# The first norm of a Mamba and gated-MLP layer on Trainium2, formed with channels instead of tokens in the partitions

## The reference, cut to what matters

```python
# x: 32 sequences x 256 tokens x 128 channels
def attn(x):                                     # a selective scan (Mamba)
    xz = x @ W_in.T;  x_ssm, z = split(xz, 2)    # 256 channels each
    x_ssm = silu(causal_conv4(x_ssm) + conv_b)
    proj = x_ssm @ W_x.T                         # B (16), C (16), one step
    dt = softplus(proj[..., -1:] * W_dt[:, 0] + b_dt)
    # h[d, n] = exp(dt * A) * h + x * dt * B[n];  y[d] = sum_n h[d, n] * C[n]
    y = (scan + x_ssm * D_param) * silu(z)
    return y @ W_out.T
x = layernorm(x + attn(x))                       # no gain, no offset, eps 1e-5
def ffn(x):
    h = silu(x @ w1.T * s1) * (x @ w2.T * s2)    # 128 -> 512
    h = gelu(h @ h1.T * t1);  h = gelu(h @ h2.T * t2)
    return h @ w3.T * s3                         # 512 -> 128
out = layernorm(x + ffn(x))
```

## Time and profile before

| | |
|---|---|
| time, median of 3 runs | 1022.49 us (1021.69 to 1024.41) |
| the profiled execution: its own time | 1023.24 us |
| its span | 1021.5 us |
| TensorE products, busy | 964.2 us, 94% |
| TensorE weight loads, busy | 427.3 us, 42% |
| VectorE busy | 933.3 us, 91% |
| ScalarE busy | 895.5 us, 88% |
| POOL busy | 877.9 us, 86% |
| granted TensorE clock, mean | 0.977 of full; 1.00 from 120 us on |

### The profile page before, as it was taken

How to read it: one execution, slowest core, us unless ns; L and a number is a source line. 1 busy time by engine, 2 the same in 40 slices (tenths; PEclk the granted TensorE clock), 3 DMA queues, 4 the chain that set the end, 5 groups by cost and what they waited for, 6 DMA issues and landing times.

```text
span 1021.5 us, 13699 instructions
## 1 busy us (share of the span) xinstructions
PE 964.2 (94%) x3874; PEld 427.3 (42%) x3874; DVE 933.3 (91%) x1117; ACT 895.5 (88%) x1496; POOL 877.9 (86%) x529
## 2 busy tenths in 40 slices
PE   7947899999999999999999999999999999999998
PEld 3213344353444435353443435344443535334454
DVE  4799999999999999999999999999999999999500
ACT  5397899999999999999999999999999999997342
POOL 3489998989999898999999898999989899988420
PEclk8687999999999999999999999999999999999999
DMA  7959394884939496693949679493949769393000
GB/s 223 249 172 276 108 290 119 221 226 130 275 100 280 111 265 177 172 268 95 273 105 268 157 207 239 120 273 103 291 109 241 203 152 267 97 275 90 0 12 11
DMA packets 110717, 185.18 MB, mean 181 GB/s; under 512 B 12976, under 2 KB 23728, under 8 KB 110640
## 3 DMA queue, kind: packets, MB, share of 16 engines
q1 hardware_dynamic: 110112, 183.98, 67.9%
q10 hardware_dynamic: 528, 0.32, 0.1%
HBM read 162.23 MB, written 22.02 MB: 180 GB/s over the span
## 4 chain that ended last, share of the span: by engine, by line
issue 35%; DVE 33%; ACT 15%; PE 10%; POOL 6%; DMA 0%; DVEq 0%; POOLq 0%; ACTq 0%; SPq 0%
DVE hb L861 18%; DVE U L850 13%; ACT dA L515 6%; PE GY L947 5%; POOL pb L407 3%; ACT L515 2%; ACT L618 2%; ACT hid L618 1%; ACT X L524 1%; PE GY L938 1%; DVE conv L790 1%; DVE x L806 1%; PE GY L1003 1%; ACT GY L611 1%; POOL xds L397 1%
## 5 line engine op out<-in xcount | busy, mean ns | idle before, releaser
L407 POOL TENSOR_TENSOR pb<-hb,crep 128x1024 f32<-128x1024 f32 x256 | 602.1, 2362 | 50.9 <-DVE hb L861 46.5
L861 DVE TENSOR_TENSOR_SCAN hb<-dA,U 128x512 f32<-128x512 f32 x512 | 594.7, 1204 | 0.0
L515 ACT ACTIVATE dA<-dtr,negA 128x510 f32<-128x510 f32 x500 | 323.2, 714 | 8.2 <-DVE hb L861 7.0
L850 DVE TENSOR_TENSOR U<-X,xdr 128x512 f32<-128x512 f32 x500 | 320.0, 688 | 6.9 <-ACT X L524 5.0
L947 PE MATMUL GY<-g,h_sb 128*128 128x512 f32 x512 | 234.2, 601 | 0.0
L947 PE MATMUL GY<-hid,h_sb 128*128 128x512 f32 x512 | 228.3, 599 | 0.9 <-ACT g L760 0.7
L947 PEld LDWEIGHTS GY<-g,h_sb 128*128 128x128 f32 x512 | 93.5, 190 | 138.2 <-issue 138.2
L947 PEld LDWEIGHTS GY<-hid,h_sb 128*128 128x128 f32 x512 | 93.9, 190 | 135.7 <-issue 125.4
L938 PE MATMUL GY<-pb,sel_sb 128*32 128x512 f32 x1024 | 140.2, 620 | 8.0 <-POOL pb L407 7.9
L469 POOL TENSOR_TENSOR hid<-hid,g 128x512 f32<-128x512 f32 x64 | 80.8, 1276 | 8.9 <-ACT g L760 8.4
L951 PE MATMUL GY<-x1T,w_sb 128*128 128x512 f32 x128 | 68.6, 618 | 0.0
(11 more groups left out here) (136 smaller groups left out, 1061.0 us busy)
## 6 DMA issues: line engine op xcount, KB each, us to landing
dtr<-scr_dt SPq DMA_DIRECT2D x252, 256.0 KB, 8.1
xdr<-scr_xd SPq DMA_DIRECT2D x252, 256.0 KB, 7.7
brep<-scr_rows SPq DMA_DIRECT2D x32, 256.0 KB, 7.0
crep<-scr_rows SPq DMA_DIRECT2D x32, 256.0 KB, 8.8
scr_dt<-dts SPq DMA_DIRECT2D x32, 256.0 KB, 4.8
scr_xd<-xds SPq DMA_DIRECT2D x32, 256.0 KB, 4.9
xres<-xT_d SPq DMA_DIRECT2D x16, 256.0 KB, 9.8
xT_sb<-xT_d SPq DMA_DIRECT2D x15, 256.0 KB, 4.3
```

The source lines that it names most:

```text
L407: nc.gpsimd.tensor_tensor(pb[:, qs:qs + 2, :], hb[:, hs:hs + 2, :], crep[:, b % 2, g:g + 1, :].to_broadcast([P, 2, TB]), ALU.mult).then_in ...
L515: nc.scalar.activation(halves(dA[:, decay_slot(b, u), :])[:, :, 1:SEQ], halves(BREP[q] if by_product(b, k) else dtr[:, slot, q, :])[:, :, ...
L850: nc.vector.tensor_tensor(U[i][:], X[:], xdr[:, slot, q + i, :], ALU.mult).then_inc(s_u, 1)
L861: nc.vector.tensor_tensor_scan(hb[:, 2 * (v % H_PAIRS) + i, :], dA[:, decay_slot(j, u), :], U[i][:], 0.0, ALU.mult, ALU.add).then_inc(s_h, 1)
```

## The change

The output projection leaves channels in the partitions and tokens in the columns: the constant and the weights become the stationary operand, 3 products of 512 columns. ScalarE squares the bank in one operation into xn (scaled so that the sum is a mean). TensorE multiplies xn by a 128 x 128 matrix of ones (a single column read 128 times), which leaves the mean of squares of each token in all partitions of the bank BVAR = G2. ScalarE forms exp(-0.5 * ln(var + eps)) in two operations into xn, and VectorE multiplies the bank BOUT by xn straight into x1T (`norm1`, at v=6). The squares by tile, the power on POOL, the transposes and the copy of x1T are gone.

With it the order moves in these places. ScalarE: the GELU of the second hidden layer is taken as m=0,1 and m=2 at v=1 and m=3 at v=4; the X copy of v=3 stands ahead of the two decays; the second z copy moves from v=5 to v=4; an explicit load of the set with logarithm and exp stands at v=4 where a next block exists. TensorE: `down` is split, its first quarter stands ahead of the sum by ones, which waits for the second z copy, because z and the sum share the bank G2.

```diff
         gT = sb("gT", [P, NC, TB])
-        x1 = sb("x1", [P, NT, DM])
-
-        wout_raw = x1[:].rearrange("p a b -> p (a b)")[:, 0:DI]
-        diagD = x1[:].rearrange("p (a c) b -> p a c b", a=2)[:, 1, :, :]
+        xn, ones = sb("xn", [P, TB]), sb("ones", [P, 1])
+
+        wout_raw = xn[:, 0:DI]
+        diagD = xn[:, DI:].rearrange("p (c b) -> p c b", c=NC)
         rep_sb = gT[:, 1, 0:PARITIES * P].rearrange("p (e m) -> p e m", e=PARITIES)
...
         s_gate, s_op = sem("s_gate"), sem("s_op")
-        s_var1, s_rs1, s_x1, s_x1t, s_x1c = sem("s_var1"), sem("s_rs1"), sem("s_x1"), sem("s_x1t"), sem("s_x1c")
+        s_sq, s_var1, s_ln1, s_rs1, s_x1 = sem("s_sq"), sem("s_var1"), sem("s_ln1"), sem("s_rs1"), sem("s_x1")
         s_ga, s_sg, s_up, s_upc, s_hid = sem("s_ga"), sem("s_sg"), sem("s_up"), sem("s_upc"), sem("s_hid")
...
         BZ = G2
-        BOUT, BX1, BW3 = Y1, Y1, G0
+        BOUT, BVAR, BW3 = Y1, G2, G0
         BGATE = (G2, G1, Y1, G2)
...
         BH1_2 = (GY[:, 0:2, :], GY[:, 2:4, :])
-        BH2_2 = (GY[:, 1:3, :], GY[:, 0:2, :])
+        BH2_2 = (GY[:, 1:3, :],)
...
             nc.gpsimd.memset(eps[:], EPS).then_inc(s_zero, 1)
+            nc.gpsimd.memset(ones[:], 1.0).then_inc(s_one, 1)
             pool.wait_ge(s_win, 16)
...
                 for v in range(STEPS):
-                    if v == 3 and back:
-                        rsqrt(var1, ve1, rs1, s_var1, F + 1, s_rs1, 2 * F + 2)
                     if v == 7 and j == NB + 1:
...
                         softplus_logs(A, 0)
+                    if v == 3 and scan and j > 0:
+                        fill_X(j, 1)
                     for u in (2 * v + AHEAD, 2 * v + AHEAD + 1):
...
                             gelu(g1, BH1[m], s_h1, s_g1, F, m, 1)
-                    if v == 3 and scan and j > 0:
-                        fill_X(j, 1)
                     if v == 3 and back:
                         act.wait_ge(s_op, F + 1)
-                        variances(x1, lambda t: tile_of(BOUT, t), var1, range(NT), s_var1)
+                        nc.scalar.activation(xn[:], BOUT, ACT.Square, scale=DM ** -0.5).then_inc(s_sq, 1)
                     if v == 8 and scan and j > 0:
...
                             gelu(g2, flat(BH2_2[0]), s_h2, s_g2, T, 0, 2)
+                            gelu(g2, BH2[2], s_h2, s_g2, T, 2, 1)
                         else:
...
                     if v == 4 and tail:
-                        if scan:
-                            gelu(g2, flat(BH2_2[1]), s_h2, s_g2, T, 2, 2)
-                        else:
-                            for m in (2, 3):
-                                gelu(g2, BH2[m], s_h2, s_g2, T, m, 1)
+                        for m in ((3,) if scan else (2, 3)):
+                            gelu(g2, BH2[m], s_h2, s_g2, T, m, 1)
+                    if v == 4 and back and front:
+                        copy_z(A, 1)
+                    if v == 4 and back:
+                        if front:
+                            act.preload_act_table_set("natural_log_exp_and_others")
+                        if j == 1:
+                            act.wait_ge(s_zero, 3)
+                        act.wait_ge(s_var1, F + 1)
+                        nc.scalar.activation(xn[:], BVAR, ACT.Ln, bias=eps[:, 0:1]).then_inc(s_ln1, 1)
+                        act.wait_ge(s_ln1, F + 1)
+                        nc.scalar.activation(xn[:], xn[:], ACT.Exp, scale=-0.5).then_inc(s_rs1, 1)
                     if v == 5 and front and not back:
...
                         act.preload_act_table_set("natural_log_exp_and_others")
-                    if v == 5 and front:
+                    if v == 5 and front and not back:
                         copy_z(A, 1)
-                    if v == 5 and back:
-                        act.wait_ge(s_x1t, F + 1)
-                        nc.scalar.activation(x1T[:, F % 2, :], BX1, ACT.Copy).then_inc(s_x1c, 1)
                     if v == 6:
...
+            def norm1(b):
+                dve.wait_ge(s_rs1, b + 1)
+                nc.vector.tensor_tensor(x1T[:, b % 2, :], BOUT, xn[:], ALU.mult).then_inc(s_x1, 1)
+
             def scaled(o, bank, rs, s_rs, n_rs):
...
                     if scan:
-                        if v == 5 and back:
-                            scaled(x1, BOUT, rs1, s_rs1, 2 * F + 2).then_inc(s_x1, 1)
                         k, q = divmod(2 * v, GT)
...
                                 nc.vector.tensor_tensor(U[i][:], X[:], xdr[:, slot, q + i, :], ALU.mult).then_inc(s_u, 1)
+                        if v == 6 and back:
+                            norm1(F)
                         if v == 9 and tail:
...
                     elif v == 5 and back and not scan:
-                        scaled(x1, BOUT, rs1, s_rs1, 2 * F + 2).then_inc(s_x1, 1)
+                        norm1(F)
                     elif v == 7 and tail and not scan and j <= NB:
...
-            def down(b):
+            def down(b, ks):
                 pe.wait_ge(s_w3c, 1)
-                pe.wait_ge(s_g2, 4 * b + 4)
-                for k in range(NH):
+                for k in ks:
+                    pe.wait_ge(s_g2, 4 * b + k + 1)
                     for t in range(NT):
...
                                                 start=False, stop=(k == NH - 1), skip_group_check=True)
-                last.then_inc(s_w3, 1)
+                if NH - 1 in ks:
+                    last.then_inc(s_w3, 1)
...
                 pe.wait_ge(s_gate, 2 * b + 2)
-                for t in range(NT):
-                    nc.tensor.matmul(tile_of(BOUT, t), tile_of(xres[:], t), cent[:], start=(t == 0), stop=False, skip_group_check=True)
-                for t in range(NT):
-                    for c in range(NC):
-                        last = nc.tensor.matmul(tile_of(BOUT, t), tile_of(gT[:, c, :], t), wout_sb[:, c, :],
-                                                start=False, stop=(c == NC - 1), skip_group_check=True)
+                nc.tensor.matmul(BOUT, cent[:], xres[:], start=True, stop=False)
+                for c in range(NC):
+                    last = nc.tensor.matmul(BOUT, wout_sb[:, c, :], gT[:, c, :], start=False, stop=(c == NC - 1))
                 last.then_inc(s_op, 1)
-            def turn_x1(b):
-                pe.wait_ge(s_x1, b + 1)
-                for t in range(NT):
-                    last = nc.tensor.transpose(tile_of(BX1, t), x1[:, t, :], ident[:])
-                last.then_inc(s_x1t, 1)
+            def sum_squares(b):
+
+                pe.wait_ge(s_sq, b + 1)
+                nc.tensor.matmul(BVAR, ones[:].to_broadcast([P, P]), xn[:], start=True, stop=True).then_inc(s_var1, 1)
...
                         z_proj(A, 1)
-                    if v == 4 and back:
-                        turn_x1(F)
                     if v == 4 and tail:
...
                     if v == 4 and tail and j <= NB:
-                        down(T)
+                        down(T, range(0, 1))
+                    if v == 4 and back:
+                        if front:
+                            pe.wait_ge(s_zc, 2 * A + 2)
+                        else:
+                            pe.wait_ge(s_g2, 4 * T + 2)
+                        pe.wait_ge(s_one, 1)
+                        sum_squares(F)
+                    if v == 4 and tail and j <= NB:
+                        down(T, range(1, NH))
                     if v == 12 and intake and not back:
...
                     if v == 6 and back:
-                        pe.wait_ge(s_x1c, F + 1)
-                        if front:
-                            pe.wait_ge(s_zc, 2 * A + 2)
+                        pe.wait_ge(s_x1, F + 1)
                         if j == 1:
...
                         gate_proj(F, 0)
```

More of the change, by code:

```diff
@@ L128, in build @@
         w3_raw = hid[:, 3, :]
-        var1, ve1, rs1 = sb("var1", [P, NT]), sb("ve1", [P, NT]), sb("rs1", [P, NT])
         var2, ve2, rs2 = sb("var2", [P, NT]), sb("ve2", [P, NT]), sb("rs2", [P, NT])
@@ L144, in build @@
         s_warm = sem("s_warm")
+        s_one = sem("s_one")
         s_zero, s_aexp, s_aneg = sem("s_zero"), sem("s_aexp"), sem("s_aneg")
```

## The result

In runs taken side by side the kernel before took 1022.87 us (median of 4, 1021.69 to 1024.41), the changed one **1030.09 us** (median of 4, 1029.25 to 1030.31). The ratio is 1.0063, 95% interval 1.0043 to 1.0082: slower, by more than the 0.3% named in the prediction. The forecast of 1026.4 us had the direction. The time lies outside the forecast's own 1024.8 to 1028.2; it lies in the stated 1018.5 to 1031 only because that range was stretched for rival D, which did not occur. That the range held is luck: the growth of the profiled execution, +6.9 us, is nearly twice the forecast +3.9.

The account below looks back on a forecast made before the run. A ScalarE-TensorE loop of 58.48 us was taken as the bound. 13 periods x 0.27 = 3.5, plus 0.1 ahead of them and 0.3 at the end, gave +3.9: 1026.4 us, own range 1024.8 to 1028.2, stated range 1018.5 to 1031.

Parts of the forecast that it names:

- rival D: In the periods the sum by ones comes after the table load, so ScalarE waits before the logarithm: +4.6, 1031 us; chance 0.15.
- ScalarE's list, +0.32 per period: ScalarE from v=1 to v=6, ahead of the gate's first SiLU: added and removed operations sum to 0.32 us more issue time.
- Place two: Handover from the gate's first SiLU on ScalarE to TensorE's second up projection: tight, about 0.05 us to spare.
- place one: Handover from ScalarE's GELU, ending at 513.05, to TensorE's tail transposes at 513.11: tight; alone it would give back 0.5 us.
- Rival B: ScalarE's addition misses the loop, TensorE's 0.5 us counts, VectorE's 57.94 sets the period: -7.0, 1015.5 us; chance 0.15.
- rival C: Slack of 0.2 to 0.3 us hidden behind place two absorbs the addition; period stays, 1022.5 to 1024 us; chance 0.17.
- VectorE's idle piece: Sign in each period: VectorE idle 0.7 to 0.8 us in one piece before the U behind the X copy.
- TensorE's ahead of the second up projection: Sign in each period: TensorE idle 0.6 to 0.8 us while the second up projection waits for the gate's first SiLU.
- round 1, "I put 0.1 on it": Block ahead of the periods, without tail: ScalarE waits for scans anyway, x1T comes later by VectorE's order; +0.1 us.
- The end, +0.3: Last round's gate, TensorE alone the path: begins at 977.6 instead of 977.33; the logarithm's own table load just hidden.

Follow-up runs that it names:

- The two copy runs: Kernel before plus one unused 128x512 ScalarE copy per period: ahead of the gate's first SiLU 1029.72 us, just ahead of the h1 GELU 1022.39 us.
- the control with the moved SiLU: Kernel before with the convolution's SiLU moved on ScalarE from ahead of the gate's first SiLU to behind its second: 1026.84 us, ratio 1.0032.

## Why the prediction was half right

- **ScalarE's list, +0.32 per period.** Measured +0.29 on the SiLU and +0.24 on the period (0.27): 12 periods give 2.9 us against the 3.5 summed over 13. The terms held: logarithm 687 ns and exp 630 ns, as the nearest rows had them, the two together 1.27 us (1.28), the square 0.48 in place of 1.00 (508.91 - 507.91 before, 513.70 - 513.22 after). ScalarE's groups by form (columns as there):

```profile
L731 ACT ACTIVATE xn<-GY,eps 128x512 f32<-128x512 f32 x16 | 11.0, 687 | 0.5 <-PE GY L1005 0.3
L733 ACT ACTIVATE xn<-xn 128x512 f32<-128x512 f32 x16 | 10.1, 630 | 0.5
```

- **Place two binds; in the changed kernel place one does not.** TensorE reached the gate 0.4 us earlier in its frame, as forecast, and nothing came of it. The two copy runs show place two directly; whether place one was as tight before the change, the control with the moved SiLU did not tell. Rival B (gain) had the right 0.4 to 0.5 us on TensorE and the wrong place, and its condition, logarithm and exp in under 1.0 us, did not hold; rival C (hidden slack) is out with +0.42 for a copy of 0.48; D is out with no wait ahead of the logarithm.
- **VectorE's idle piece** was put at 0.7 to 0.8 and is 0.88; TensorE's ahead of the second up projection at 0.6 to 0.8 and is 0.39. The weights' wait, 1.22, was the clearer sign.
- **The step that failed: round 1, "I put 0.1 on it".** It is 2.46, the largest single part of what the forecast missed. The prediction was right that the later x1T itself is absorbed. It did not ask what TensorE does meanwhile: what the tail's products fill in rounds 2 to 14 is empty in round 1 for 4.00 us, and the price is the halved clock under the gate and up projections. The evidence stood in the trace of before, in that round's rows of TensorE: 2.87 us idle ahead of the transposes, and a granted clock of 0.50 behind it.
- **The end, +0.3.** The step counted "a table load of its own" and there are two; from projection to gate it is +1.10, of which 0.93 is the second load. With one load it is +0.17 (0.26 was put on TensorE's path). All of the 1.10 reaches the end of the execution: from the gate on it is 44.17 before and 44.22 after. The Trainium skill (ScalarE: Activation LUTs, Table sets: the hidden batching unit) counts one load for a logarithm followed by an exp, since one set has both; the trace shows two where no set is named, at 979.20 and 981.48, and one where it is. The 1.38 us of drain that the Trainium skill (ScalarE: Activation LUTs, What ACT_TABLE_LOAD costs) adds to each switch is not seen: function follows function with 1.28 and a few hundredths between, at 517.91 to 519.21 and 981.48 to 982.77.
- **The start, +0.6.** Not forecast, and no larger than what comes without a change: the output projection of round 1 began anywhere from 91.45 to 93.78 us in variants of the changed kernel whose code ahead of it is the same, and from 92.16 to 93.36 in such variants of the kernel before. Each was profiled once. The cause of that spread stays open.

## What to carry to other kernels

Price a longer dependent chain in the rounds where the pipe fills and empties as well as in its steady state: what is covered there is bare at the ends. Look there at TensorE's granted clock, too, and at which products run while it is low: here the wait of 4.00 us cost nothing by itself, and the slow products behind it cost 2.46. When work is added to an engine that does not seem to bind, ask what stands ahead of the next instruction that another engine waits for; the same copy cost 0.42 us a period on one side of it and nothing on the other. Moving an instruction out of one tight place pays only as far as the next list that it stands ahead of; try it with the control kernel too, since it may pay in one and cost in the other.

## What was not expected of the hardware

- TensorE's granted clock was at 0.50 behind idle pieces of 4.00 and 3.06 us in round 1, and behind the piece of 2.87 us of the kernel before as well. What it cost hung on what ran then. After the change the first four products of gate and up took 6.5 us (109.13 to 115.63) instead of the 3.6 of the run with four products ahead of them (108.68 to 112.31), and the round grew by 2.46. Before, a sum group and four transposes ran slowly (103.91 to 106.81), the gate and up products behind them took 1.25 and 1.02, and the round lost nothing.
- ScalarE's logarithm from PSUM with a column as bias costs what an identity of the same form does: 687 against 688 ns.
- Two functions that one table holds got a load each, 1.28 us, where the program named no table.
